# A graph network's edge sort: twelve of 28 blocks scattered by POOL's transfers, the layers' small additions apart, eight row buffers

## The chip, the cores and the metric

The kernel runs on one core of one Trainium2 chip. The metric is the time of one execution on the device, in microseconds.

## The reference

```python
# x: 12500 x 64, edges: 400000 with src, dst (sorted by dst), edge_weight
# attention layer
a = einsum('nd,hde->nhe', h, Wh)
attn = softmax(sum(a * h[:, None, :], -1) / sqrt(d), axis=0)
neigh = segment_sum(h[src][:, None, :] * attn[src][:, :, None], dst, n)
x = layernorm(x + elu(neigh.reshape(n, -1) @ weight))
# three message layers, then x = layernorm(x + h)
ef = concatenate([nf[src], nf[dst], traj[:, None]], -1)
msg = leaky_relu(ef @ We.T + be)
red = segment_sum(msg, dst, n)
h = leaky_relu(concatenate([nf, red], -1) @ Wn.T + bn)
```

## The kernel before

All gathers by node are made with one-hot matmuls on windows of 128 nodes (98 windows, `NW`). For that the edges are first put in the order of the source's window, and later, in quads of four slots, in the order of the target's window. The program runs through these stages one after the other.

**Sort** (the block at L482 to L757). The 3125 tiles of 128 edges are cut into 28 blocks of 115 tiles (the last has 20), and these into lots of five tiles, 23 lots a block, 625 in all. In a block every edge gets a rank, its place among 16384 slots of the block when it is ordered by window, with each window's part rounded up to runs of 16. SP loads a block's rows; PE turns them, ACT casts them (L513); DVE makes the fields (`fields_of`, L627). Then, by lots, DVE writes the one-hots of windows and segments (L667, L669), PE counts them (L554, L556) and, 29 lots later, adds up the ranks (L581 to L588), which DVE reads with a maximum (L701, 30 lots behind the one-hots) and, at the end of each group of eight lots, splits into column and row (`places`, L705). Ten lots later still (`LAG_GRID` 40) comes the grid: DVE writes one-hots of column and row (L721, L722) and four products of the column one-hot with fields (L725), ACT two more products for every tile (L521, `weigh`), and PE multiplies row one-hots with these (L602), so that a 128x128 grid of three fields fills in two banks. DVE reads it (L733, `read_grid`) and SP stores it in `runs` (L502). POOL does nothing in this stage. The order on each engine is that of the loops `for lot in steps_of`; semaphores count lots.

**Preparation** (L758 to L1217): where each run goes, gathers of runs by POOL (L1034), the fields of the slots (`make_meta`, L1037), the attention's scores.

**Source phase** (`source_phase`, L1257), once for the attention and once for each layer: 960 groups of 512 slots, two groups a transfer. SP loads the one-hots (`hits_s`, L1293) and POOL the side rows (L1331) three transfers ahead, ACT copies the group's window of the table (L1347), PE makes the products (L1368, L1373), DVE copies a bank into one of four row buffers `made` (L1396), and SP stores a buffer of two groups in `rows` (L1301). DVE may write into a buffer when its last store has landed. Each engine's loop has eight groups a turn (`laps`, L1224).

**Target phase** (`first_target_phase`, L1430, and `target_phase`, L1553, for the layers): 976 groups of 128 quads. POOL gathers the quads' rows (L1457, L1581). In a layer SP loads one-hots of two groups (L1591), PE makes the target's part (L1622), DVE adds it to the quads (`add`, L1654), applies the leaky rectifier (`leaky`, L1658), splits the message into three bfloat16 pieces (`less`, L1662, `split`, L1666), PE sums by node (L1426), and DVE adds the sums into `hr` (`keep`, L1673), one small addition a group, whose window comes from a register that is loaded at L1245. Each `keep` waits until the one before it has been written. Between layers stands `between`, L1755.

```python
            for p in range(pairs + 3):
                if p < pairs:
                    add(p)
                if 1 <= p <= pairs:
                    less(p - 1)
                if p < pairs:
                    leaky(p)
                if 1 <= p <= pairs:
                    split(p - 1)
                if p >= 3:
                    keep(2 * p - 6)
                    keep(2 * p - 5)
```

## Time and profile before

| | |
|---|---|
| median of 3 runs | 13272.0 us (13263.73 to 13275.16) |
| the profiled execution | 13268.24 us, its span 13266.9 us |
| busy: PE, DVE | 8804.1 us, 10738.3 us |
| busy: ACT, POOL | 5614.5 us, 5614.8 us |
| mean granted TensorE clock | 0.885 |
| DMA | 1931.77 MB in 1720140 packets, mean 146 GB/s |

Engines: PE is TensorE (PEld its weight loads), DVE VectorE, ACT ScalarE, POOL GpSimd, SP SyncE. A row of a group of instructions gives line, engine, operation, output and inputs, their number, then busy time and mean time of one, then the idle time of the engine before them and what ended it. A row of the timeline gives start, duration, engine, line, operation and, in brackets, the idle time before it.

### The profile page before, as it was taken

The numbers are of one execution on the slowest core, as the hardware profiler recorded it, in microseconds if no ns is written. First come the engines' busy times: TensorE is split into PE (matmuls) and PEld (weight loads), VectorE is DVE, ScalarE is ACT, GpSimd is POOL, SyncE is SP. The second block draws the span as 40 slices with busy tenths as digits, with TensorE's granted clock in tenths as the row PEclk, the third lists the DMA queues.
The fourth block names the chain that finished last, engine by engine and source line by source line (L and its number), as shares of the span: only waits on it lengthen the run. The fifth ranks groups of instructions, "written<-read, shape, count | busy, mean of one in ns | idle before, by whom it ended". The sixth has DMA issues, their size and how long they took to land. (4 is left out here: it accounts for less than half of the span.)

```text
span 13266.9 us, 519123 instructions
## 1 busy us (share of the span) xinstructions
PE 8804.1 (66%) x172644; PEld 7365.0 (56%) x172644; DVE 10738.3 (81%) x26542; ACT 5614.5 (42%) x15578; POOL 5614.8 (42%) x6333
## 2 busy tenths in 40 slices
PE   6777777766377666656765555777555567756556
PEld 4555555543366655556665555566555556655554
DVE  8999999986377799985569998555999965589997
ACT  4666666661133388764432222344222234422222
POOL 0000000017522377752346666234666633366663
PEclk9999999985555588868999999899999989999998
DMA  1000000002488767776875556587555558855555
GB/s 36 5 5 5 5 5 5 4 7 48 122 246 245 211 195 195 195 152 184 269 227 171 172 172 162 142 261 246 171 171 171 170 112 265 269 182 172 171 172 108
DMA packets 1720140, 1931.77 MB, mean 146 GB/s; under 512 B 256050, under 2 KB 1577028, under 8 KB 1719140
## 3 DMA queue, kind: packets, MB, share of 16 engines
q1 hardware_dynamic: 1458065, 1370.73, 34.0%
q0 software_dynamic: 261120, 548.82, 17.1%
q8 instruction: 238, 3.90, 0.1%
q10 hardware_dynamic: 304, 4.93, 0.1%
q14 instruction: 413, 3.38, 0.1%
HBM read 1202.74 MB, written 725.45 MB: 145 GB/s over the span
## 5 line engine op out<-in xcount | busy, mean ns | idle before, releaser
L1581 POOL DMA_INDIRECT work<-rows,quad_at x2928 | 3091.6, 1056 | 1490.4 <-DVE work L1654 1000.2
L1426 PE MATMUL bank<-work 128*128 128x64 bf16 x46848 | 2073.8, 199 | 1358.8 <-DVE hr L1673 1349.1
L1426 PEld LDWEIGHTS bank<-work 128*128 128x128 fp8e4 (+1 forms) x46848 | 1846.7, 102 | 1515.1 <-issue 1462.5
L1606 ACT COPY work<-tabs 128x192 bf16 x2928 | 1028.8, 351 | 3556.3 <-PE bank L1622 3231.4
L1396 DVE COPY work<-bank 128x256 f32<-128x256 f32 (+1 forms) x3840 | 1551.8, 422 | 1107.5 <-DMA rows<-work 625.1
L1373 PE MATMUL bank<-work 128*128 128x64 bf16 x46080 | 2412.7, 203 | 0.5 <-issue 0.5
L521 ACT ACTIVATE work<-work,tabs 128x128 bf16<-128x128 bf16 x6250 | 1919.2, 427 | 932.7 <-DVE work L721 932.7
L1347 ACT COPY work<-tabs 128x192 bf16 x3840 | 1349.0, 351 | 2108.0 <-PE bank L1373 1605.3
L1373 PEld LDWEIGHTS bank<-work 128*128 128x128 fp8e4 x46080 | 2167.6, 104 | 0.6 <-issue 0.6
L1331 POOL DMA_DIRECT2D side<-meta x1920 | 1071.5, 558 | 2301.9 <-PE bank L1373 2083.9
L1368 PE MATMUL bank<-wtraj,side 128*128 128x64 bf16 x11520 | 1558.1, 195 | 555.7 <-ACT work L1347 252.1
L1622 PE MATMUL bank<-work 128*128 128x64 bf16 x35136 | 1304.2, 195 | 541.8 <-DMA work<-hits_g 305.4
L1368 PEld LDWEIGHTS bank<-wtraj,side 128*128 128x128 bf16 x11520 | 1130.1, 98 | 764.3 <-DVE work L1396 519.6
L1622 PEld LDWEIGHTS bank<-work 128*128 128x128 fp8e4 x35136 | 1167.0, 99 | 673.2 <-issue 613.0
L602 PE MATMUL bank<-work 128*128 128x384 bf16 x9375 | 1290.6, 291 | 38.6 <-ACT work L521 38.6
L725 DVE TENSOR_TENSOR work<-work,tabs 128x768 bf16<-128x768 bf16 x2500 | 1222.0, 549 | 0.0
L778 POOL MEMSET tabs<- 128x976 f32 x1 | 0.9, 916 | 2871.5 <-DMA runs<-work 2871.5
L1457 POOL DMA_INDIRECT work<-rows,quad_at x976 | 984.6, 1009 | 416.4 <-PE bank L1426 228.5
L1654 DVE TENSOR_TENSOR work<-bank,work 128x512 f32<-128x512 f32 x1464 | 1012.8, 692 | 137.3 <-PE bank L1622 102.2
L602 PEld LDWEIGHTS bank<-work 128*128 128x128 bf16 x9375 | 825.1, 102 | 384.9 <-issue 56.9
L1658 DVE SCALAR_TENSOR_TENSOR work<-work 128x512 f32<-128x512 f32 x1464 | 1001.4, 684 | 0.1
L1666 DVE TENSOR_TENSOR work<-work 128x512 bf16<-128x512 f32 x1464 | 1000.9, 684 | 0.1
(324 smaller groups left out, 13996.5 us busy)
## 6 DMA issues: line engine op xcount, KB each, us to landing
work<-hits_g SPq DMA_DIRECT2D x1464, 256.0 KB
rows<-work SPq DMA_DIRECT2D x1440, 256.0 KB, 3.4
work<-hits_s SPq DMA_DIRECT2D x1440, 128.0 KB, 3.2
hits_g<-work SPq DMA_DIRECT2D x976, 128.0 KB
rows<-work SPq DMA_DIRECT2D x480, 260.0 KB, 4.9
work<-rows,quad_at POOLq DMA_INDIRECT x3904
work<-meta_src SPq DMA_DIRECT2D x480, 128.0 KB, 4.2
hits_s<-work SPq DMA_DIRECT2D x480, 128.0 KB, 4.6
```

The costliest lines, as they stand in the source:

```text
L521: last = sca.activation(values[lot % 3][:, f, j // 2, :, j % 2], of_tile(hit_col[lot % 3], j), ACT.Copy, scale=of[name][:, t:t + 1])
L602: last = ten.matmul(to[:, f * P:3 * P].rearrange("p (f c) -> p f c", c=P), of_tile(hit_row[lot % 3], j), v[:, fields[0]:fields[1], j // 2, ...
L725: last = vec.tensor_tensor(values[at][:, f, :, :, :], hit_col[at], twos(lot, name, P), ALU.mult)
L1331: pool.dma_start(side[0:high - low, n % 4, :, :], meta[bass.ds(l * GROUP_LOT, GROUP_LOT), low:high, :].rearrange("g r s -> r g s")).then_i ...
L1347: sca.copy(window[q % 8].unsqueeze(1), tabs[:, 0, bass.ds(w, 1), :]).then_inc(s_window, 1)
L1368: ten.matmul(home, beside, wtraj[:, :], start=True, stop=False, skip_group_check=True)
L1373: last = ten.matmul(home, hits[n][:, q % GROUP_LOT, slots], window[q % 8][:, k * D:(k + 1) * D], start=False, stop=k == 2, skip_group_chec ...
L1396: vec.tensor_copy(made[n][:, q % GROUP_LOT, :], bank[q % 8][:, 0:QUAD * width]).then_inc(s_read, 1)
L1426: last = ten.matmul(to[:, 0:D], hits_of(j), piece_of(j), start=j == 0 and k == 0, stop=j == QUAD - 1 and k == 2, skip_group_check=True)
L1581: pool.indirect_dma_start(quads[g // 2 % (GATHERED // 2)][:, half(g)], None, table, bass.IndirectOffsetOnAxis(ap=quad_at[:, g:g + 1], axis ...
L1606: sca.copy(window[q % 4].unsqueeze(1), tabs[:, 1, bass.ds(w, 1), :]).then_inc(s_window, 1)
L1622: last = ten.matmul(to[:, j * D:(j + 1) * D], hits_t[:, j * P:(j + 1) * P], window[q % 4][:, k * D:(k + 1) * D], start=k == 0, stop=k == 2 ...
```

## The change

1. Blocks 0, 2, ... 22 (`by_pool`) do not go through the grid. DVE writes their fields as records (source low part + 1, target, weight) in one of four record buffers and turns the ranks into slot numbers with one instruction per group of places. POOL then issues one indirect transfer of 128 records of 12 bytes per tile into a table of that block in DRAM, `runs_of`, and, when the next such block is through, one transfer that copies the table into `runs`. SP fills these twelve tables with blanks first. The other sixteen blocks use the grid as before, counted among themselves (`grid_no`). All engines wait at the end for the grid's stores and for `s_moved`.
2. A run's layout is now slot by slot (`e f`) instead of field by field (`f e`), in the grid read, the blanks and `make_meta`.
3. In the source phases there are eight row buffers (`MADE`) and sixteen groups a turn.
4. In the target phases of the layers the two small additions stand apart.

```diff
+    by_pool = lambda b: b % 2 == 0 and b < 24
+    RECORDS = 4
+    record = [room.cut(3 * BT).rearrange("p (t f) -> p t f", f=3) for _ in range(RECORDS)]
+    slot = [room.cut(BT).bitcast(I32) for _ in range(RECORDS)]
+    runs_of = {b: dram(f"runs_of_{b}", [BLOCK_RUNS, 3 * RUN], F32) for b in pool_blocks}
+    @block.gpsimd
+    def _(pool):
+        pool.wait_ge(*edges_here)
+        pool.wait_ge(s_blanked, 16 * len(pool_blocks))
+        def move(k):
+            b = pool_blocks[k]
+            pool.wait_ge(s_scattered[k % RECORDS], 16 * BT * (k // RECORDS + 1))
+            pool.dma_start(in_rows(runs[b * BLOCK_RUNS:(b + 1) * BLOCK_RUNS, :]), in_rows(runs_of[b])).then_inc(s_moved, 16)
+        for n, (first, end) in enumerate(place_groups):
+            b = group_block[n]
+            if by_pool(b):
+                k = pool_blocks.index(b)
+                way = k % RECORDS
+                to = runs_of[b].rearrange("r (e f) -> (r e) f", f=3)
+                pool.wait_ge(s_slots, kind_no(n) + 1)
+                for t in range(tile(first, 0), tile(end - 1, LOT - 1) + 1):
+                    pool.indirect_dma_start(to, bass.IndirectOffsetOnAxis(ap=slot[way][:, t:t + 1], axis=0),
+                                            record[way][:, t, :], None).then_inc(s_scattered[way], 16)
+                if end == blocks[b][1] and k >= 1:
+                    move(k - 1)
+        move(len(pool_blocks) - 1)
...
     def _(syn):
         syn.wait_ge(*edges_here)
+        syn.wait_ge(*blanks_ok)
+        for b in pool_blocks:
+            syn.dma_start(in_rows(runs_of[b]), blanks.rearrange("p s f -> p (s f)")).then_inc(s_blanked, 16)
...
         def fields_of(b):
+            if by_pool(b):
...
+                at_least(vec, s_scattered[k % RECORDS], 16 * BT * (k // RECORDS))
+                vec.tensor_copy(record[k % RECORDS][:, :, 1], turn_bank[:, BT:2 * BT])
+                vec.tensor_copy(record[k % RECORDS][:, :, 2], weight)
+                vec.tensor_scalar(record[k % RECORDS][:, :, 0], low_i[:, 0:BT], 1.0, None, ALU.add)
...
         def places(n):
             vec.wait_ge(s_rank, end)
+            if by_pool(b):
+                vec.tensor_scalar(slot[pool_blocks.index(b) % RECORDS][:, a:z], rank_f[b % 2][:, a:z], -float(BIG), None,
+                                  ALU.add).then_inc(s_slots, 1)
+                return
...
-            if here(lot - LAG_GRID):
+            if in_grid(lot - LAG_GRID):
                 spread(lot - LAG_GRID)
...
     for e in (nc.vector, nc.scalar, nc.tensor, nc.sync, nc.gpsimd):
         for n in range(2):
-            e.wait_ge(s_stored[n], 16 * NB // 2)
+            e.wait_ge(s_stored[n], 16 * len(grid_blocks) // 2)
+        e.wait_ge(s_moved, 16 * len(pool_blocks))
...
+        MADE = 8
+        around = MADE * GROUP_LOT
-        made = [room.cut(GROUP_LOT * QUAD * width).rearrange("p (g c) -> p g c", g=GROUP_LOT) for _ in range(4)]
+        made = [room.cut(GROUP_LOT * QUAD * width).rearrange("p (g c) -> p g c", g=GROUP_LOT) for _ in range(MADE)]
-            laps(vec, NS, step)
+            laps(vec, NS, step, around)
...
                     add(p)
+                if p >= 3:
+                    keep(2 * p - 6)
                 if 1 <= p <= pairs:
                     less(p - 1)
+                if p >= 3:
+                    keep(2 * p - 5)
                 if p < pairs:
                     leaky(p)
                 if 1 <= p <= pairs:
                     split(p - 1)
-                if p >= 3:
-                    keep(2 * p - 6)
-                    keep(2 * p - 5)
```

The order on DVE in the target phase of a layer, before the change; `TENSOR_LOAD win_g` is the register load of a small addition, `ISA` belongs to its address:

```order
 L1673 TENSOR_TENSOR hr<-hr,bank 128x64
 L1245 TENSOR_LOAD win_g
 L1673 ISA
 L1673 TENSOR_TENSOR hr<-hr,bank 128x64
 L1654 TENSOR_TENSOR work<-bank,work 128x512
 L1662 TENSOR_TENSOR work<-work 128x512
 L1658 SCALAR_TENSOR_TENSOR work<-work 128x512
 L1666 TENSOR_TENSOR work<-work 128x512
```

The same place after the change (L1736 is the addition of the quads, L1744, L1740 and L1748 are the old L1662, L1658 and L1666, L1755 is the small addition):

```order
 L1736 TENSOR_TENSOR work<-bank,work 128x512
 L1322 TENSOR_LOAD win_g
 L1755 ISA
 L1755 TENSOR_TENSOR hr<-hr,bank 128x64
 L1744 TENSOR_TENSOR work<-work 128x512
 L1322 TENSOR_LOAD win_g
 L1755 ISA
 L1755 TENSOR_TENSOR hr<-hr,bank 128x64
 L1740 SCALAR_TENSOR_TENSOR work<-work 128x512
 L1748 TENSOR_TENSOR work<-work 128x512
```

One of the two additions and its load moved ahead of the subtraction, the other behind it.

The order on POOL in the sort after the change, where before it had no instruction between L369 and L778; L530 is the scatter of one tile's records (230 for blocks 0 and 2 together), L520 the move of a finished block:

```order
 L369 MEMSET marker 1x1
 L416 MEMSET tabs 128x128x2
 L417 MEMSET tabs 128x128
 L511 UNCONDITIONAL_BRANCH
 L530 DMA runs_of<-tabs 16384x3 x230
 L520 DMA runs<-runs_of 16x3072
 L530 DMA runs_of<-tabs 16384x3 x115
 L520 DMA runs<-runs_of 16x3072
```

A block's 115 scatters stand between two moves, and the move of a block stands behind the scatters of the next one.

## Rows read from the trace of the kernel before

**Rows 1.** The page: busy time of engines, and DVE's busy tenths in 40 slices

```profile
PE 8804.1 (66%) x172644; PEld 7365.0 (56%) x172644; DVE 10738.3 (81%) x26542; ACT 5614.5 (42%) x15578; POOL 5614.8 (42%) x6333
...
DVE  8999999986377799985569998555999965589997
```

**Rows 2.** Busy time by stage; last columns granted clock, DMA share, GB/s

```profile
54.00:2919.00 2865.00, 2117.62 (x23346) 1592.93 (x23346) 2840.62 (x6737) 1925.91 (x6276) 0.52 (x1) 0.95 0.02 5
3491.00:4531.00 1040.00, 782.51 (x15331) 715.27 (x15328) 739.57 (x1916) 333.94 (x951) 279.40 (x476) 0.55 0.85 245
...
6087.00:6820.00 733.00, 560.84 (x15343) 493.26 (x15340) 379.42 (x960) 334.50 (x952) 260.87 (x476) 0.99 0.87 268
6832.00:8323.00 1491.00, 878.56 (x22937) 784.90 (x22937) 1355.45 (x2872) 335.52 (x955) 1016.05 (x963) 0.98 0.61 169
8474.00:9227.00 753.00, 569.22 (x15341) 497.38 (x15338) 386.04 (x960) 334.43 (x952) 260.96 (x476) 0.99 0.85 261
...
10882.00:11622.00 740.00, 569.41 (x15337) 500.48 (x15334) 381.39 (x960) 334.23 (x952) 260.89 (x476) 0.99 0.86 266
```

**Rows 3.** Timeline of DVE in the sort, before the grid's first lot

```profile
90.72 0.67 DVE L701 TENSOR_REDUCE work<-bank 128x5 f32<-128x490 f32 x1 [1.13 <-PE bank L588]
...
93.76 0.67 DVE L701 TENSOR_REDUCE work<-bank 128x5 f32<-128x490 f32 x1
```

**Rows 4.** Timeline of DVE in the sort, a lot with grid work

```profile
155.50 0.66 DVE L701 TENSOR_REDUCE work<-bank 128x5 f32<-128x490 f32 x1
...
157.01 1.96 DVE L725 TENSOR_TENSOR work<-work,tabs 128x768 bf16<-128x768 bf16 x4
...
159.72 0.66 DVE L701 TENSOR_REDUCE work<-bank 128x5 f32<-128x490 f32 x1
```

**Rows 5.** Grouped instructions: POOL's indirect transfers

```profile
L1581 POOL DMA_INDIRECT work<-rows,quad_at x2928 | 3091.6, 1056 | 1490.4 <-DVE work L1654 1000.2 <-issue 490.2
...
L1191 POOL DMA_INDIRECT marks_g<-later_home x98 | 116.4, 1188 | 33.9 <-issue 33.9
L898 POOL DMA_INDIRECT marks_s<-tabs x28 | 27.1, 966 | 19.0 <-DVE tabs L906 10.7 <-issue 8.2
```

**Rows 6.** Timeline of DVE in a layer's target phase, one iteration

```profile
7500.80 0.68 DVE L1662 TENSOR_TENSOR work<-work 128x512 f32<-128x512 f32 x1
7501.40 0.69 DVE L1658 SCALAR_TENSOR_TENSOR work<-work 128x512 f32<-128x512 f32 x1
7502.00 0.69 DVE L1666 TENSOR_TENSOR work<-work 128x512 bf16<-128x512 f32 x1
7502.60 0.21 DVE L1673 TENSOR_TENSOR hr<-hr,bank 128x64 f32 x1
7503.04 0.22 DVE L1673 TENSOR_TENSOR hr<-hr,bank 128x64 f32 x1 [0.22 <-DVE hr L1673]
...
7503.85 0.68 DVE L1662 TENSOR_TENSOR work<-work 128x512 f32<-128x512 f32 x1
```

**Rows 7.** Timeline of POOL in the same iteration

```profile
7501.15 1.16 POOL L1581 DMA_INDIRECT work<-rows,quad_at  x1 [0.63 <-DVE work L1654]
7502.62 0.96 POOL L1581 DMA_INDIRECT work<-rows,quad_at  x1 [0.30 <-issue]
```

**Rows 8.** Grouped instructions: small additions, and PE's target part in the layers

```profile
L1622 PE MATMUL bank<-work 128*128 128x64 bf16 x35136 | 1304.2, 195 | 541.8 <-DMA work<-hits_g 305.4 <-DVE work L1654 198.2 <-issue 3.9
...
L1673 DVE TENSOR_TENSOR hr<-hr,bank 128x64 f32 x2928 | 634.4, 217 | 337.1 <-DVE hr L1673 337.1
```

**Rows 9.** The layers' source phases: grouped instructions, and a window as in rows 2

```profile
L1396 DVE COPY work<-bank 128x256 f32<-128x256 f32 x2880 | 1147.4, 422 | 1104.7 <-DMA rows<-work 625.1 <-PE bank L1373 444.0
L1368 PEld LDWEIGHTS bank<-wtraj,side 128*128 128x128 bf16 x11520 | 1130.1, 98 | 764.3 <-DVE work L1396 519.6 <-issue 155.2 <-ACT work L1347 42.4
...
6294.00:6306.00 12.00, 9.27 (x290) 8.61 (x286) 6.80 (x18) 5.62 (x16) 4.91 (x9) 1.00 0.95 300
```

**Rows 10.** Grouped instructions: the grid read

```profile
L733 DVE TENSOR_SCALAR work<-bank 128x128 f32<-128x128 f32 x84 | 19.0, 279 | 3.4 <-PE bank L602 3.4
```

More of the change, by code:

```diff
@@ L450, in build @@
     s_stored = [sort(f"grid_stored{n}") for n in range(2)]
+    s_blanked, s_slots, s_moved = sort("blanked"), sort("slots"), sort("moved")
+    s_scattered = [sort(f"scattered{n}") for n in range(RECORDS)]
     place_groups = []
@@ L480, in ends_block, with in_grid, grid_no, kind_no @@
         return block_of(lot) if here(lot) and lot + 1 == blocks[block_of(lot)][1] else None
+    def in_grid(lot):
+        return here(lot) and not by_pool(block_of(lot))
+    def grid_no(lot):
+        return sum(1 for k in range(lot) if in_grid(k))
+    def kind_no(n):
+        return sum(1 for k in range(n) if by_pool(group_block[k]) == by_pool(group_block[n]))
     block = nc.Block()
     block.__enter__()
+    @block.gpsimd
[19 more added lines that the diff above has]
+        move(len(pool_blocks) - 1)
     @block.sync
@@ L617, in _ @@
                 rank(lot - LAG_RANK + 1)
-            if here(lot - LAG_GRID - 1):
+            if in_grid(lot - LAG_GRID - 1):
                 grid(lot - LAG_GRID - 1)
@@ L629, in fields_of @@
             vec.wait_ge(s_turned, b + 1)
-            if b >= 4:
-                vec.wait_ge(s_grid, blocks[b - 4][1])
+            if b >= 4 and not by_pool(b - 4):
+                vec.wait_ge(s_grid, grid_no(blocks[b - 4][1]))
             wide = lambda ap: ap[:, 0:2 * BT].rearrange("p (f t) -> p f t", f=2)[:, :, 0:n]
@@ L751, in _ @@
                     places(group_ends[lot - LAG_RANK])
-            if here(lot - LAG_GRID):
+            if in_grid(lot - LAG_GRID):
                 spread(lot - LAG_GRID)
-            if (b := ends_block(lot, LAG_GRID + 2)) is not None:
+            if (b := ends_block(lot, LAG_GRID + 2)) is not None and not by_pool(b):
                 read_grid(b)
@@ L1222, in build, with laps @@
     LAP = 8
-    def laps(engine, count, step):
-        for q in range(LAP):
+    def laps(engine, count, step, size=LAP):
+        for q in range(size):
             step(q, q, 0)
-        with engine.Fori(1, count // LAP - 1) as i:
-            for q in range(LAP):
-                step(i * LAP + q, q, i)
-        for g in range(count - LAP, count):
-            step(g, g % LAP, g // LAP)
+        with engine.Fori(1, count // size - 1) as i:
+            for q in range(size):
+                step(i * size + q, q, i)
+        for g in range(count - size, count):
+            step(g, g % size, g // size)
     serial = itertools.count()
@@ L1318, in _ @@
                 load(l, l)
[L1319 removed]
+            laps(syn, NS, step, around)
             for l in range(lots - 2, lots):
@@ L1375, in step @@
                 last.then_inc(s_rows, 1)
-            laps(ten, NS, step)
+            laps(ten, NS, step, around)
         @block.vector
```

110 lines of the change are left out of this document (66 added, 44 removed).

## The prediction, made before the changed kernel was run

> **What bounds the kernel now.** I read the engines' shares first, then busy time by stage, then the grouped instructions of the stages that the change touches, then single iterations in the timeline. Over the whole span DVE is busiest, 81%, but its share by slice runs from 9 down to 3 [rows 1], so no engine bounds everything. The stages differ [rows 2]:
>
> - The sort, from 54 to 2919 us, has DVE busy 2840.6 of 2865.0 us, POOL with one instruction and DMA at a share of 0.02. It is DVE's alone.
> - Each of the three layers' source phases takes 733 to 753 us. DVE is busy only about half of it and PE three quarters, and DMA has a share of 0.85 to 0.87 at 261 to 268 GB/s: transfers and waits for them.
> - Each target phase takes about 1490 us, with DVE busy 1355.45 of 1491. It is DVE's again, with gaps.
>
> **The sort on DVE.** Before the grid starts, a lot costs DVE two one-hots and one rank read: the rank reads at 90.72 and 93.76 stand two lots apart, so 1.52 us a lot [rows 3]. With the grid's two one-hots and four products the next rank read comes 4.22 us later (155.50 to 159.72), and the four products alone fill 1.96 us [rows 4]. A block scattered by POOL drops these six, so a lot saves 4.22 - 1.52 = 2.70 us. Twelve blocks of 23 lots are 276 lots: 745 us. Each such block also drops the three instructions of its grid read, nine of twelve on places (three in each of three groups) and five of thirteen on fields. At the grid read's 0.279 us [rows 10] these 17 are at most 4.7 us a block, at least 0; they overlap in part and I take 2.5, in all 30 us. Against it stand twelve blank fills that are queued on SP ahead of the first block's loads; 12 x 196 KB at the 245 GB/s that DMA moved in the first source phase [rows 2] are 10 us. So DVE would end the sort 745 + 30 - 10 = 765 us earlier, at 2919 - 765 = 2154 us. ACT (ten weighings a lot) and PE (the grid's matmuls) only lose work there; DVE, busy 2840.6 of 2865.0 us, hardly waits for them, so that is worth nothing.
>
> **The sort on POOL.** POOL gets 12 x 115 = 1380 scatters of 128 records of 12 bytes. The trace has no such scatter. Nearest are the marks: 98 records take 0.966 us and about 0.30 us until the next, 125 records take 1.188 us and 33.9/98 = 0.35 us; the gathers of 128 rows take 1.056 us in the mean [rows 5]. That brackets one scatter between 0.95 + 0.30 = 1.25 us and 1.19 + 0.35 = 1.54 us when nothing disturbs it. Something does: in the target phase the gather that starts while DVE runs L1662 takes 1.16 us, the one that starts beside L1666's end and L1673 takes 0.96 us [rows 6, 7]. The first gets going when L1662 ends, although L1658 has already started, so it waits for one DVE instruction with two SBUF inputs, 0.2 us here. In the sort DVE runs such instructions nearly without a break, each 0.55 us long and begun every 0.47 us, so a scatter waits 0 to 0.43 us, some 0.2 us in the middle. I take 0.96 + 0.20 + 0.30 = 1.46 us less a little for the rank reads, which read PSUM, so 1.44 us; ends 1.25 and 1.54 + 0.2 = 1.74 us. POOL's first slots are ready when eight lots are ranked, near 105 to 110 us. Then it ends at 110 + 1380 x 1.44 + 12 us for the twelve moves of finished blocks = 2109 us. DVE's 2154 is later, so **DVE still bounds the sort**, by only 45 us. At 1.25 us POOL ends at 1847 and nothing changes; at 1.74 us it ends at 2523, and the sort saves 396 instead of 765 us. POOL becomes the bound from (2154 - 122) / 1380 = 1.47 us on. Four record buffers let POOL lag three of its blocks before DVE's field step waits, so DVE need not stop. The new waits on POOL have nothing else queued behind them, and the moves wait for scatters of the block before, long landed. DMA had a share of 0.02, so the records' traffic is hidden.
>
> The new layout of runs makes the later DVE reads step 12 bytes; they stepped before too. Priced at 0, bounds -5 to +20 us for some 100 instructions of the preparation stage.
>
> **The layers' small additions.** In a target iteration the first addition into hr starts at 7502.60 and lasts 0.21, the second starts at 7503.04: 0.22 us are idle, released by the first one [rows 6]. Over 2928 additions that idle time is 337.1 us [rows 8]. After the change a subtraction of 0.6 us lies between them, as the order of the instructions shows, and the window's register load still has an instruction to run under. The iteration goes from 3.05 (7500.80 to 7503.85) to 2.82 us; 1464 x 0.23 = 337 us. What may be late next: a pair's two gathers now need 1.16 + 0.30 + 0.96 + 0.30 = 2.72 us [rows 7], and if both meet a blocking instruction 2.92; and the loads of hits_g, for which PE waits 305.4 us already [rows 8], are issued after a scatter that is now released by the last split of an iteration instead of the first addition. I give back 37 us: **300 us**, ends 0 and 337.
>
> **Eight row buffers.** In the source phases DVE waits 625.1 us for stores of rows to land [rows 9], 208 us of about 740 a phase. That is not the gain, because DMA is at 0.87. After a stall, 12 us ran at a share of 0.95 and 300 GB/s [rows 9], against 268 in the mean. So at most 733 x (1 - 268/300) = 78 us a phase, 235 in all, at least 0. I take halfway to 300, 284 GB/s: 733 x (1 - 268/284) = 41 us a phase, 124 in all. The loops' bodies double too, which halves the turns. PE's weight loads of the three phases wait 155.2 us for nothing that the profile shows [rows 9]; half of it, 78, is the most that fewer turns can give, 0 the least, and I take 26. Together **150 us**. The first source phase waits little for stores of rows; 0.
>
> **Sum.** 765 + 300 + 150 = 1215 us off the profiled execution's own 13268.2 us (span 13266.9): 12053, say **12050 us**. The median of the runs shown, 13272.0, lies 4 us above that execution, which changes nothing.
>
> **The rivals.**
> *POOL bounds the sort.* For it: my 1.44 and the crossing at 1.47 us nearly touch, and a scatter of 125 records took 1.54. Against: 98 records and gathers of 128 rows run at 1.26. At 1.60 us POOL ends at 122 + 2208 = 2330, 176 us after DVE: 12050 + 176 = 12226, about 12230 us.
> *Layers give little.* DMA at 0.87 is already the ceiling, and in the target phase half of the 300 us comes back as waits for hits_g or for gathers. For it: PE's 305.4 us and the thin POOL margin. Against: the 300 GB/s stretch. Then 12050 + 150 + 150 = 12350 us.
> *Slower.* A scatter waits not for one DVE instruction but for the whole unbroken run, so that one gets through per rank read. A lot with grid work is 4.22 us, one without 1.52; at 3.0 us a scatter POOL ends the sort at 122 + 4140 = 4262, 1343 later than now, and the total is 13268 + 1343 - 450 = 14160 us. It turns the sign from (2919 + 450 - 122) / 1380 = 2.35 us a scatter on. Against it is the gather that got in between L1662 and L1658 [rows 6, 7]. The Trainium skill's page "SBUF — State Buffer", section "Who interferes with whom", says that a VectorE instruction with two SBUF inputs and a GpSimd instruction that reads SBUF exclude each other, and that the loser is fully blocked. The trace agrees on the blocking, and shows it ending with the one instruction.
> *It doesn't do what it says.* The scatter's slots would come so late that grid and scatter run one after the other, or the gap between additions is the register load's: no gain over 0.2%.
>
> **How the numbers follow.** Forecast 50%, POOL-bound 20%, layers give little 24%, slower 4%, nothing 2%. A measurement of this kernel can tell about 0.2%, 27 us. Faster 0.94, same 0.02, slower 0.04. The range: down by 85 us for the source phases' end, 37 for the target phases', and some 60 for the small terms, 11870; up it takes in POOL at 1.60 us and the poor layers (12350) with 100 us of POOL's lag on top, 12450.
>
> **What would show it.** Right: the sort ends near 2150 us with DVE at 9 throughout, POOL's scatters 1.15 us each, 1.44 us apart, done some tens of us before DVE; in the target phase no idle time released by the other addition and 2.82 us between two additions from the bank; in the source phases the wait of DVE for rows gone, DMA over 0.9, some 690 us each. Wrong: a last wait of the sort for POOL's moves with DVE idle; DVE in the target phase waiting for PE behind hits_g; source phases still 733 us with PE waiting for its loads.

## The result, and the profile after

The changed kernel takes 12440.2 us (median of 4 runs, 12430.95 to 12460.75) against 13271.2 us (4 runs, 13263.73 to 13275.16) of the kernel before: a ratio of 0.9377, 95% interval 0.936 to 0.9393. The profiled execution took 12460.75 us, its span is 12459.6 us. That is 807 us less than the profiled execution before. I had forecast 1215 us less. The median lies in my range, 10 us below its upper end of 12450; the profiled execution lies 11 us above it.

The page, engines' busy time and the slices, answers to [rows 1]:

```profile
PE 8132.3 (65%) x168504; PEld 6910.0 (55%) x168504; DVE 9842.5 (79%) x24682; ACT 4777.9 (38%) x12818; POOL 7654.0 (61%) x7727
...
DVE  8997779634677799986569999555999965589997
POOL 5888888877322477762347777233777733367774
```

DVE's row begins with 8997779 where it stood at 9 before, and POOL is at 8 over the same slices: the sort is no longer DVE's alone. Busy time by stage (sort, first source phase, a source and a target phase of the first layer, the two other source phases), as in [rows 2]:

```profile
54.00:2574.00 2520.00, 1592.80 (x19209) 1244.60 (x19209) 2049.08 (x4877) 1080.03 (x3519) 2007.66 (x1393) 0.87 0.04 6
...
3149.00:4195.00 1046.00, 775.32 (x15344) 710.46 (x15342) 739.61 (x1916) 334.31 (x952) 280.13 (x476) 0.57 0.85 243
5751.00:6469.00 718.00, 556.16 (x15347) 494.06 (x15344) 405.95 (x959) 334.51 (x952) 262.06 (x476) 0.99 0.88 274
6480.00:7858.00 1378.00, 854.65 (x23291) 770.15 (x23288) 1313.94 (x2914) 340.29 (x968) 1029.71 (x972) 0.97 0.66 185
7984.00:8715.00 731.00, 570.28 (x15336) 500.99 (x15334) 406.25 (x959) 334.35 (x952) 262.04 (x476) 0.98 0.87 269
10231.00:10958.00 727.00, 569.31 (x15347) 500.23 (x15344) 407.33 (x960) 334.50 (x952) 262.05 (x476) 0.99 0.87 271
```

From the first and last instructions of each stage in the two traces:

| stage | before, us | after, us | difference | forecast |
|---|---|---|---|---|
| end of the sort | 2918.5 | 2573.7 | -344.8 | -765 |
| three source phases of the layers | 2224.3 | 2175.9 | -48.4 | -150 |
| three target phases of the layers (first to last large addition) | 4554.0 | 4134.2 | -419.8 | -300 |
| all the rest | | | +5.5 | 0 |

So three terms of the sum were off, and they partly cancel: 420 us too much in the sort, 102 too much in the source phases, 120 too little in the target phases.

**The sort after.** The scatters as one line's instructions (smallest, median and largest duration in ns, first and last start):

```profile
L530 POOL DMA_INDIRECT runs_of<-tabs x1380: 956/1007/5911, 108.5 to 2568.0; - x198
its engine sat idle before it (us, times) until:
  issue: 454.2, 1379
  DVE tabs L781: 61.4, 1
who waited for it (us, times):
  DVE tabs L699: 204.7, 5
```

POOL scatters from 108.5 us up to the end of the sort. It waited for DVE once, 61.4 us before the first scatter, and then only its own 0.3 us between two (3 us where a move stands between them): it is the bound. The median, 1.007 us, is below the 1.16 I had forecast; the mean is 2000.5 / 1380 = 1.450 us, because there is a second kind. DVE waits too, 204.7 us in five places, for a record buffer that POOL has not emptied. At the end of the sort it stands idle for 200.75 us:

```profile
2575.98 0.07 DVE L866 MEMSET tabs<- 1x16 f32 x1 [200.75 <-POOL tabs L859]
```

So DVE was through at 2375.2 us, and without the 204.7 us of waiting it would have been at 2170.5. Here is the second kind, in the timeline of POOL and, for the same time, of DVE (start, duration, engine, line):

```profile
2098.91 3.92 POOL L530 DMA_INDIRECT runs_of<-tabs  x1 [0.30 <-issue]
2103.13 3.92 POOL L530 DMA_INDIRECT runs_of<-tabs  x1 [0.30 <-issue]
```

```profile
2098.26 0.55 DVE L796 TENSOR_TENSOR work<-lane_pairs,tabs 128x768 bf16<-128x768 bf16 x1
2098.73 0.55 DVE L797 TENSOR_TENSOR work<-lane_pairs,tabs 128x768 bf16<-128x768 bf16 x1
2099.20 1.96 DVE L800 TENSOR_TENSOR work<-work,tabs 128x768 bf16<-128x768 bf16 x4
2101.07 0.46 DVE L737 TENSOR_TENSOR tabs<-lane_pairs,tabs 128x588 bf16<-128x588 bf16 x1
2101.45 0.55 DVE L739 TENSOR_TENSOR work<-lane_pairs,tabs 128x750 bf16<-128x750 bf16 x1
2101.91 0.67 DVE L771 TENSOR_REDUCE work<-bank 128x5 f32<-128x490 f32 x1
```

The scatter that starts at 2098.91, 0.18 us into the second one-hot (L797), is done at 2102.83. That is 0.83 us after the last instruction with two SBUF inputs, L739, has ended (2101.45 + 0.55 = 2102.00). One gets through per lot of 4.22 us. Other scatters end 0.83 us after the one DVE instruction that they met: 1.10 us is the usual length of one that starts in a later L800. Counted over the records of L530, 206 of 1380 took more than 2 us, 3.765 us in the mean, and 1174 took 1.043 us in the mean. Each of the 206 ends 0.83 to 0.88 us after the last instruction with two SBUF inputs of an unbroken run (L739, or the last L800 in lots without one-hots), none after one in the middle of a run. The longest, 5.91 us, met a run of twelve, two lots' grid work with no reduction between. The 206 cost 206 x (3.765 - 1.043) = 561 us of POOL's time. Without them POOL would have been done near 2007 us, ahead of DVE.

**The target phases after**, the timeline of DVE over one iteration, answers to [rows 6]:

```profile
7001.78 0.68 DVE L1736 TENSOR_TENSOR work<-bank,work 128x512 f32<-128x512 f32 x1
7002.38 0.21 DVE L1755 TENSOR_TENSOR hr<-hr,bank 128x64 f32 x1
7002.51 0.68 DVE L1744 TENSOR_TENSOR work<-work 128x512 f32<-128x512 f32 x1
7003.11 0.21 DVE L1755 TENSOR_TENSOR hr<-hr,bank 128x64 f32 x1
7003.24 0.68 DVE L1740 SCALAR_TENSOR_TENSOR work<-work 128x512 f32<-128x512 f32 x1
```

and the grouped instructions, to [rows 8]:

```profile
L1704 PE MATMUL bank<-work 128*128 128x64 bf16 x35136 | 1300.6, 195 | 1033.9 <-DMA work<-hits_g 1017.9 <-issue 11.0 <-DVE work L1736 3.4
...
L1736 DVE TENSOR_TENSOR work<-bank,work 128x512 f32<-128x512 f32 x1464 | 1005.0, 686 | 219.8 <-PE bank L1704 194.5 <-DMA work<-rows,quad_at 13.2 <-PE bank L1508 0.9
...
L1755 DVE TENSOR_TENSOR hr<-hr,bank 128x64 f32 x2928 | 617.9, 211 | 11.1 <-PE bank L1508 6.4 <-DVE hr L1755 0.9
```

The wait of 337.1 us is gone. The next instruction also starts 0.13 us after a small addition, not 0.21: its last 0.08 us now lie under the next one. PE's wait for hits_g has grown from 305.4 to 1017.9 us, and 194.5 us of it reach DVE.

**The source phases after**, answers to [rows 9]:

```profile
L1449 PE MATMUL bank<-wtraj,side 128*128 128x64 bf16 x11520 | 1555.3, 196 | 514.6 <-ACT work L1427 264.8 <-DVE work L1478 113.2 <-DMA side<-meta 79.6
L1449 PEld LDWEIGHTS bank<-wtraj,side 128*128 128x128 bf16 x11520 | 1132.4, 98 | 715.7 <-DVE work L1478 270.3 <-ACT work L1427 264.2 <-issue 115.2
```

DVE's wait for rows to land (625.1 us) is gone, but PE's weight loads sit idle nearly as long as before (715.7 against 764.3 us), now partly for ACT's window copies.

### The profile page after: what moved, and what is told of

It is laid out like the page before. It is cut to its first block and busy times, and to the rows that moved or that the text cites. A ratio compares the mean times of both kernels' runs of the same rounds, so it can differ in the third digit from the quotient of the medians.

```text
span 12459.6 us, 502768 instructions
## 1 busy us (share of the span) xinstructions
PE 8132.3 (65%) x168504; PEld 6910.0 (55%) x168504; DVE 9842.5 (79%) x24682; ACT 4777.9 (38%) x12818; POOL 7654.0 (61%) x7727
## 5 line engine op out<-in xcount | busy, mean ns | idle before, releaser
L1454 PE MATMUL bank<-work 128*128 128x64 bf16 x46080 | 2405.8, 203 | 0.2 <-issue 0.2
L1478 DVE COPY work<-bank 128x256 f32<-128x256 f32 (+1 forms) x3840 | 1625.9, 424 | 986.8 <-PE bank L1454 895.2
L1508 PE MATMUL bank<-work 128*128 128x64 bf16 x46848 | 1943.9, 199 | 574.4 <-DVE work L1748 568.6
L530 POOL DMA_INDIRECT runs_of<-tabs x1380 | 2000.5, 1450 | 515.6 <-issue 454.2
L1508 PEld LDWEIGHTS bank<-work 128*128 128x128 fp8e4 (+1 forms) x46848 | 1747.0, 102 | 696.0 <-issue 673.9
L1704 PE MATMUL bank<-work 128*128 128x64 bf16 x35136 | 1300.6, 195 | 1033.9 <-DMA work<-hits_g 1017.9
L577 ACT ACTIVATE work<-work,tabs 128x128 bf16<-128x128 bf16 x3490 | 1071.1, 427 | 1219.9 <-DVE work L796 1219.9
L1449 PEld LDWEIGHTS bank<-wtraj,side 128*128 128x128 bf16 x11520 | 1132.4, 98 | 715.7 <-DVE work L1478 270.3
L1736 DVE TENSOR_TENSOR work<-bank,work 128x512 f32<-128x512 f32 x1464 | 1005.0, 686 | 219.8 <-PE bank L1704 194.5
L1744 DVE TENSOR_TENSOR work<-work 128x512 f32<-128x512 f32 x1464 | 1000.7, 684 | 1.3
L1740 DVE SCALAR_TENSOR_TENSOR work<-work 128x512 f32<-128x512 f32 x1464 | 1000.1, 683 | 0.1
L1748 DVE TENSOR_TENSOR work<-work 128x512 bf16<-128x512 f32 x1464 | 999.3, 683 | 0.0
L1451 PE MATMUL bank<-ones_b,side 128*128 128x1 bf16 x3840 | 692.6, 187 | 452.2 <-DVE work L1470 201.3
L610 PE MATMUL bank<-work,tabs 128*98 128x125 bf16 x3125 | 431.9, 231 | 683.6 <-DVE work L739 676.2
```

The source lines that it names most:

```text
L530: pool.indirect_dma_start(to, bass.IndirectOffsetOnAxis(ap=slot[way][:, t:t + 1], axis=0), record[way][:, t, :], None).then_inc(s_scattere ...
L577: last = sca.activation(values[n % 3][:, f, j // 2, :, j % 2], of_tile(hit_col[n % 3], j), ACT.Copy, scale=of[name][:, t:t + 1])
L1449: ten.matmul(home, beside, wtraj[:, :], start=True, stop=False, skip_group_check=True)
L1454: last = ten.matmul(home, hits[n][:, q % GROUP_LOT, slots], window[q % 8][:, k * D:(k + 1) * D], start=False, stop=k == 2, skip_group_chec ...
L1478: vec.tensor_copy(made[n][:, q % GROUP_LOT, :], bank[q % 8][:, 0:QUAD * width]).then_inc(s_read, 1)
L1508: last = ten.matmul(to[:, 0:D], hits_of(j), piece_of(j), start=j == 0 and k == 0, stop=j == QUAD - 1 and k == 2, skip_group_check=True)
```

## The experiments

My theory after the result: POOL bounds the sort, through scatters that are held by a whole run of DVE instructions with two SBUF inputs; the target phases' gain belongs to the small additions alone; the source phases are close to what the transfers allow. Each step is tried by itself. Numbers are from one profiled execution each where no interval is given. Beside the first three kernels below the kernel before took 13255.5 us; beside the three cuts, the ten blocks and the two deeper loads 13262.7; beside the single cut, the control, the halved stores and the first combination 13319.2, 0.4% more on the chip of the same number as 13262.7, for which I have no reason; beside the last 13250.1.

**The small additions alone**, in the kernel before:

```diff
                     add(p)
+                if p >= 3:
+                    keep(2 * p - 6)
                 if 1 <= p <= pairs:
                     less(p - 1)
+                if p >= 3:
+                    keep(2 * p - 5)
...
-                if p >= 3:
-                    keep(2 * p - 6)
-                    keep(2 * p - 5)
```

> The kernel before with one part of the change alone: in the target phases of the layers the two small additions of a pair stand apart (the first behind the pair's addition, the second behind the first subtraction). If this part alone carries the gain of the target phases, each of the three falls from about 1518 to about 1378 us, as in the changed kernel, the wait of the small addition falls from 337 us to under 30 us, the sort (end at 2918), the first source phase (1040) and the layers' source phases (732 to 752) stay, and the whole is near 12,850 us. Rival: part of the 420 us comes from the rest of the change (other row buffers, other places in SBUF, rows already written when the phase begins); then the phases stay above 1420 us and the whole above 12,970 us.

Measured: 12822.0 us, 433.5 less than before. The target phases took 1375.8, 1371.3 and 1372.2 us, the small addition's wait fell to 9.5 us, the sort stayed, and the layers' source phases took 9 us less together though nothing was changed in them. Its grouped instructions show the same new wait of PE as the changed kernel:

```profile
L1622 PE MATMUL bank<-work 128*128 128x64 bf16 x35136 | 1300.6, 195 | 1018.5 <-DMA work<-hits_g 1002.9 <-issue 12.8 <-DVE work L1654 0.5
...
L1673 DVE TENSOR_TENSOR hr<-hr,bank 128x64 f32 x2928 | 613.7, 210 | 9.5 <-PE bank L1426 4.7 <-DVE hr L1673 1.2
```

So the whole gain of the target phases is this part's, and it is more than half of what the change gives.

**The eight row buffers alone**, in the kernel before:

```diff
+        MADE = 8
+        around = MADE * GROUP_LOT
-        made = [... for _ in range(4)]
+        made = [... for _ in range(MADE)]
-            laps(vec, NS, step)
+            laps(vec, NS, step, around)
```

> The kernel before with eight row buffers (and sixteen groups a turn) in the source phases, nothing else changed. If the 48 us that the layers' source phases lost belong to this part, they become 718 to 732 us each, VectorE's wait for a row buffer disappears (625 us over the program in the kernel before), the target phases stay at 1516 to 1520 us, and the whole is near 13,220 us. Rival one: VectorE's wait was on the path as I forecast, and something else in the changed kernel ate the gain; then the phases come near 690 us each and the whole near 13,120 us. Rival two: the eight buffers give nothing and the 48 us come from elsewhere; then the whole stays within 15 us of the kernel before.

Measured: 13232.6 us, 22.9 less. The layers' source phases took 711.8, 734.3 and 733.1 us, 45 us less together; the first source phase took 9 us more and the target phases 6 us more. The DMA share stands where it stood in the changed kernel, 0.86 to 0.88. The first expectation holds within some 3 us a phase: the 45 to 48 us are this part's but for the 9 us that these phases moved by themselves in the kernel above, and nothing else in the changed kernel ate a larger gain.

**A fifth of the scatters**, in the changed kernel (the counts that two waits expect fall with them):

```diff
-                for t in range(tile(first, 0), tile(end - 1, LOT - 1) + 1):
+                for t in range(tile(first, 0), tile(end - 1, LOT - 1) + 1, 5):
```

> The changed kernel, with POOL scattering only every fifth tile of each of its twelve blocks: 276 scatters instead of 1380. It leaves out four fifths of the records of these blocks. VectorE's work is the same. If POOL bounds the sort of the changed kernel, and VectorE would be done at my 2154 us, the sort ends between 2130 and 2230 us instead of at 2574, and the whole falls by the same 340 to 440 us to 12,020 to 12,110 us. Rival: it is VectorE's own term that was wrong (its instructions take longer beside the scatters, or it waits for PE or for loads), and POOL only follows; then the sort still ends after 2400 us.

Measured: 12043.2 us, sort end 2171.8 us, POOL's last scatter at 1762 us (20 of its 276 are held as well). DVE's work in the sort is that of the changed kernel (x4877 in both windows), in 402 us less:

```profile
54.00:2172.00 2118.00, 1598.93 (x19209) 1248.28 (x19209) 2045.02 (x4877) 1080.03 (x3519) 336.94 (x289) 0.94 0.03 7
```

So POOL's scatters are the whole difference, and my 2154 us for DVE was right to 18 us.

**Cuts in DVE's run.** Three memsets of two columns per grid lot, in the changed kernel:

```diff
+    gap, turns = room.cut(128), itertools.count()
+    def cut_run(vec):
+        vec.memset(gap[:, 2 * (next(turns) % 64):][:, 0:2], 0.0)
...
             vec.tensor_tensor(hit_row[at], columns(P), twos(lot, "row", P), ALU.is_equal)
+            cut_run(vec)
...
                 last = vec.tensor_tensor(values[at][:, f, :, :, :], hit_col[at], twos(lot, name, P), ALU.mult)
+                if f == 1:
+                    cut_run(vec)
             last.then_inc(s_vector_values, 1)
+            cut_run(vec)
```

> The changed kernel with three VectorE memsets of two columns in each grid lot, which stand between its instructions that read two operands from SBUF: so the unbroken run of these, some 4 us, is cut into four pieces of 0.7 to 1.5 us. Added for VectorE: 276 x 3 x about 0.06 us, some 50 us, which alone would put its own end at about 2220 us (2172 in the kernel with a fifth of the scatters). If a scatter that begins beside this run is held until the run ends (206 of 1380 take over 2 us, mostly 3.92 us), the cuts let it through earlier: few or none above 2.3 us, the mean falls from 1.45 us to 1.1 to 1.25 us, and the sort ends between 2250 and 2400 us, by 170 to 320 us earlier. Rival one: a cut by a memset frees nothing (a scatter gets through only where VectorE reads PSUM, or waits); then the long ones stay at about 200 of 3.9 to 4.1 us, and the sort ends at 2574 to 2640 us. Rival two: the long ones are a matter of POOL's own queue (a full ring, a late transfer) and have nothing to do with VectorE; then their number and length stay too, and they no longer end with VectorE's last subtraction of a lot.

Measured: 12074.5 us, sort end 2188.6 us, the last scatter issued at 2169.4; 37 scatters above 2 us. The scatters of this kernel, grouped:

```profile
L534 POOL DMA_INDIRECT runs_of<-tabs x1380 | 1597.1, 1157 | 520.6 <-issue 458.3 <-DVE tabs L785 62.3
```

The gain is larger than expected, since DVE ends the sort only 17 us after the end it had with a fifth of the scatters. The memsets are 62.8 us busy but lie partly beside their neighbours. The 37 show that such a memset does not always let a scatter through: 27 of them were held across all three, 9 across two, and all 37 end where the run ends. Is it the place of the cuts, or their number? Two more kernels ask that.

**One cut in place of three**, the middle one (behind `f == 1`):

> The changed kernel with one of the three memsets in each grid lot, the middle one, between the second and third product: the unbroken run of eight instructions becomes one of four (2.2 us) and one of four (2.1 us). If a scatter is let through at the cut, and one that begins in the first part waits at most some 2.3 us, no scatter is near 3.9 us any more except where the run is longer than a lot's, and the sort ends between 2170 and 2300 us. Rival: what frees a scatter is a short piece (a single instruction or two), and one cut leaves most of the held ones held, now for 2 to 2.5 us; then over 200 of them are above 1.6 us and the sort ends between 2300 and 2450 us.

Measured: sort end 2211.5 us, 12168.8 us in all (beside 13319.2), 65 scatters above 2 us, 34 of them above 3 us where I had expected hardly any; the end of the sort is as expected. This kernel shows a release at the cut. Timeline of POOL, and of DVE from the same lot:

```profile
252.89 2.15 POOL L534 DMA_INDIRECT runs_of<-tabs  x1 [0.30 <-issue]
```

```profile
253.19 1.49 DVE L804 TENSOR_TENSOR work<-work,tabs 128x768 bf16<-128x768 bf16 x3
254.15 0.06 DVE L453 MEMSET work<- 128x2 f32 x1
```

The second product starts 0.47 us after the first and lasts 0.55, so it ends near 254.21, where the cut is; the scatter ends at 255.04, 0.83 us later. 29 of the 65 end so, at the cut; the other 36 were held across it and end with the run. Of the 88 scatters that start 150 to 190 ns into the second one-hot, 28 end like this one, 40 end after one instruction (1.2 us), and 20 are held for 3 us or longer in spite of the cut. In the changed kernel 148 of 149 that start there are held.

**The same three memsets where the run ends anyway**, just ahead of `read_rank` (the control):

```diff
             if here(lot - LAG_RANK):
+                if in_grid(lot - LAG_GRID):
+                    for _ in range(3):
+                        cut_run(vec)
                 read_rank(lot - LAG_RANK)
```

> The changed kernel with the same three memsets of two columns in each grid lot as in the kernel with the cuts (x1047, 63 us of VectorE), but all three together just ahead of the reduction of the ranks, where the unbroken run ends anyway. If it is the place of the memsets that freed the scatters, nothing is freed here: about 200 or more of the scatters stay at 3.9 us, and the sort ends at 2560 to 2660 us. Rival: the memsets help by their mere number (they slow VectorE and shift its turns against POOL's); then the number above 2 us falls to under 100 here too, and the sort ends below 2400 us.

Measured: 12144.5 us (beside 13319.2), sort end 2188.7 us. My expectation failed and the rival held. The scatters:

```profile
L534 POOL DMA_INDIRECT runs_of<-tabs x1380: 954/1097/2476, 110.7 to 2071.8; - x198
```

Not one is held for a whole run, although the run has no cut. Timelines of POOL and of DVE for one lot:

```profile
1505.17 1.23 POOL L534 DMA_INDIRECT runs_of<-tabs  x1 [0.30 <-issue]
1506.71 1.10 POOL L534 DMA_INDIRECT runs_of<-tabs  x1 [0.31 <-issue]
1508.12 1.00 POOL L534 DMA_INDIRECT runs_of<-tabs  x1 [0.30 <-issue]
```

```profile
1503.49 0.54 DVE L743 TENSOR_TENSOR work<-lane_pairs,tabs 128x750 bf16<-128x750 bf16 x1
1503.98 0.06 DVE L453 MEMSET work<- 128x2 f32 x1
1503.98 0.66 DVE L775 TENSOR_REDUCE work<-bank 128x5 f32<-128x490 f32 x1
...
1505.02 0.55 DVE L801 TENSOR_TENSOR work<-lane_pairs,tabs 128x768 bf16<-128x768 bf16 x1
```

The scatter at 1505.17 starts 0.15 us into the second one-hot and is through after 1.23 us. POOL's pattern now repeats with the lot, three scatters each, and falls a few tens of ns earlier against DVE: of those that start in the second one-hot, 85 lie 100 to 149 ns into it, 0 held. In the changed kernel 149 lie 150 to 199 ns into it, and 148 of them are held. So a run of DVE holds a scatter only in some alignments of the two engines, and memsets get rid of the held ones in two ways: by a release at the cut, which the kernel with one cut shows, and by something that works from outside the run as well, a shift of the pattern or a change of how DVE takes up its next instruction. How much of the gain of the three cuts is the one and how much the other I can't say, and why so small a shift should decide stays open.

**Ten blocks instead of twelve** on POOL (`b < 20`), in the changed kernel:

> The changed kernel with ten of the 28 blocks on POOL instead of twelve; the two others go back to the grid. POOL: (2568 - 108) / 12 = 205 us a block, so ten end near 2160 us by themselves. VectorE: 2172 us where POOL held nothing up (a fifth of the scatters), and 69 us for each of two more grid blocks, so 2310 us. Each engine's work then fits below the other's, and VectorE is the bound: the sort ends between 2290 and 2350 us, the whole falls by 225 to 285 us to 12,155 to 12,235 us. Rival: POOL's time is no sum of its own scatters but is made by the grid lots beside it (a held scatter for each run of VectorE), and VectorE waits for record buffers in turn, so that fewer blocks on POOL help less; then the sort ends above 2400 us.

Measured: 12300.7 us, sort end 2414.2 us. Fewer scatters, and yet more of them held: 258 of 1150 above 2 us, and a higher mean:

```profile
L530 POOL DMA_INDIRECT runs_of<-tabs x1150 | 1917.8, 1668 | 439.8 <-issue 378.4
```

The 258 take 976 us, 703 us more than they would at the 1.056 us of the others; without that POOL would have been done near 1706 us, ahead of the 2310 that I had drawn up for DVE. DVE, too, waited 108.6 us for record buffers and was through at 2405; less that wait it is at 2297, as drawn up. The rival stands: POOL's price per block isn't its own, it is made by the grid lots beside it.

**Eight buffers of hits in the layers' target phases**, in the changed kernel, sixteen groups a turn:

```diff
-        hits_home = [... for _ in range(4)]
+        hits_home = [... for _ in range(DEEP)]
...
-                at_least(syn, s_sum, 2 * (p - 3), since)
+                at_least(syn, s_sum, 2 * (p - DEEP + 1), since)
...
-            for p in range(3):
+            for p in range(DEEP - 1):
```

> The changed kernel with eight instead of four buffers for the hits of a pair in the layers' target phases, loaded seven pairs ahead instead of three. If PE's 1018 us of waiting at the first product is the short lead of these loads (a load is issued when the pair three ahead of it has been summed, and lands 3 us later), most of this wait goes, and the excess at the end of each phase (45 us above the steady 2.67 us a pair) with it: each target phase falls from 1378 to 1310 to 1345 us, the whole by 100 to 200 us. Rival: the pace of 2.67 us is POOL's (two gathers of 1.33 us from start to start, no idle time), and the excess at the end is the transfers' own time, whatever their lead; then PE's wait turns into another one, the median stays at 2.67 us, and the phases stay within 15 us of 1378.

Measured: the target phases took 1342.1, 1340.9 and 1340.9 us, 110 us less together; the total, 12378.7, falls by 61.5 us and not by the 100 to 200 expected, because its sort ended at 2598.7 us (218 scatters held). PE's wait is gone, and no other took its place on PE:

```profile
L1705 PE MATMUL bank<-work 128*128 128x64 bf16 x35136 | 1307.6, 195 | 67.1 <-DMA work<-hits_g 33.6 <-issue 23.6 <-DVE work L1737 0.5
```

So the short lead of the loads was the cause. (The loop's turns were doubled in the same edit; no run has that alone. It is the wait for hits_g that went, from 1017.9 to 33.6 us.) What is left over DVE's own 1301 us a phase is 40 us.

**Eight buffers of hits and side values in the layers' source phases** (loads seven lots ahead instead of three, `hits_home` and `side` eight deep), in the changed kernel:

> The changed kernel with eight instead of four buffers for the hits and for the side values in the layers' source phases, loaded seven lots ahead instead of three. If PE waits there for loads that were issued too late, the phases fall by 20 us or more each (718 to 732 us now). Rival, which I hold likelier: PE's waits for the loads are small (some 80 us over three phases for the side values), and the pace is set by the chain of ACT's windows, PE's products and VectorE's copy, or by what the 16 DMA engines can move at a share of 0.88; then the phases stay within 10 us.

Measured: 713.0, 731.7 and 723.2 us, 8 us less together, where the small additions alone, which change nothing in them, had moved them by 9; the whole took 12455.2 us. The rival holds: the lead of these loads isn't what bounds there.

**Half of the row stores** in the second and third layer's source phases, in the changed kernel:

```diff
-                syn.dma_start(to_rows[:, bass.ds(l * GROUP_LOT, GROUP_LOT), :], made[n % MADE])
+                syn.dma_start(to_rows[:, bass.ds(l * GROUP_LOT, 1 if number > 1 else GROUP_LOT), :], made[n % MADE][...])
```

> The changed kernel, storing in the source phases of the second and third layer only one of each two groups' rows. It leaves out half of the rows that the second and third layer's target phases gather (they read older ones). If the pace of the source phases is what the 16 DMA engines can move (share 0.88, 271 to 275 GB/s now, of which the stores are the larger part), these two phases fall from 731 and 726 us to 550 to 650 us. Rival: the pace is the chain of ACT's window copy, PE's products and VectorE's copy of the sums, and the DMA engines merely keep up; then the two phases stay within 15 us of 731 and 726 while the DMA share falls.

Measured, first the layer that stores all, then the two that store half:

```profile
5808.00:6527.00 719.00, 556.23 (x15337) 496.00 (x15335) 404.96 (x959) 334.49 (x952) 260.93 (x476) 0.98 0.88 273
8050.00:8689.00 639.00, 520.27 (x15353) 480.70 (x15350) 403.37 (x960) 334.57 (x952) 260.88 (x476) 0.98 0.72 210
10215.00:10848.00 633.00, 517.73 (x15351) 476.86 (x15348) 402.98 (x960) 334.69 (x953) 260.93 (x476) 0.99 0.73 212
```

The first expectation holds (550 to 650 us). The two phases fall by about 93 us against the 731 and 726 of the changed kernel, and the share from 0.87 to 0.72: the transfers are on the path. They aren't all of it, for at a share of 0.72 the phase still takes 633 us.

**Combinations.** The first has the three cuts, the deep hits, and the moves of finished blocks on SP:

> The changed kernel with the three cuts, with the eight buffers of hits in the layers' target phases, and with the moves of POOL's finished blocks issued by SP, eight blocks later, instead of by POOL (each cost POOL a gap of 3 us). From the two kernels measured apart: 12,075 us with the cuts less 3 x 36 us of the target phases is 11,965 us. The moves: POOL ends its last scatter at 2169 us in the kernel with the cuts and VectorE is as late, so taking 36 us from POOL gives 0 to 15 us. I expect 11,950 to 11,970 us, a ratio of 0.901 to 0.903 to the kernel before. Rival: the moves on SP's queue hold back its loads of coming blocks (a move waits for the last scatter), and the sort ends later than 2188 us.

Measured: 12021.9 us (4 runs) beside 13319.2 (7 runs), ratio 0.9022 [0.9007, 0.9037]; as expected in the ratio, while the time itself is 52 us above what I had expected. The sort ends at 2188.4 us: the moves on SP gave nothing, as DVE is the bound. The second has the three memsets ahead of `read_rank`, the deep hits and the deep source loads:

> The changed kernel with the three memsets just ahead of the reduction of the ranks (the place where they were meant to free nothing, and where one scatter of 1380 took over 2 us), with the eight buffers of hits in the layers' target phases, and with the eight buffers of hits and side values in the layers' source phases; POOL keeps its moves. If the effects add up: sort end 2189 us as before with either set of memsets (VectorE is its bound, POOL's last scatter at 2072 us), target phases near 1342 us, source phases 713 to 735 us, so a ratio of 0.901 to 0.903 to the kernel before, the same as the kernel with the cuts and the deep hits within 0.1%. If the freedom from held scatters was luck of where POOL's scatters happened to start, a new layout may bring them back: then over 100 of them take more than 2 us again, and the sort ends after 2300 us.

Measured: 11932.2 us (4 runs) beside 13250.1 (7 runs), ratio 0.9009 [0.8994, 0.9024]. No scatter is above 2 us, the sort ends at 2186.6 us, the target phases take 1340.2, 1339.0 and 1339.2 us:

```profile
L534 POOL DMA_INDIRECT runs_of<-tabs x1380: 957/1099/1952, 110.1 to 2080.4; - x198
```

This kernel also narrows the open question of the control. 25 of its scatters start 150 to 159 ns into the second one-hot, and none is held; of those that start in these 10 ns, both are held in the changed kernel and 5 of 7 in the first combination. So to within 10 ns the place of the start alone does not decide.

Both beat the changed kernel (0.9377) by nearly 4%. The intervals of the two overlap.

## Why the prediction was right or wrong

The total is inside the range partly by luck: the sort lost 420 us of its forecast gain, more than the 176 + 100 us that the upper end allowed for it, and the layers, for which it took off 300 us, together gave 18 us more than forecast. Two of the signs of being wrong that I had named are in the trace: DVE idle at the end of the sort (200.75 us), and DVE waiting for PE behind hits_g (194.5 us).

- **"DVE would end the sort at 2154 us"**: right. 2171.8 us with a fifth of the scatters.
- **"A scatter waits for one DVE instruction; I take 1.44 us"**: this is the step that failed. It measured (2568.0 - 108.5) / 1379 = 1.78 us from start to start, above even my upper end of 1.74. For 1174 scatters the step was right and even too dear (1.04 + 0.30 = 1.34 us). For 206 it was wrong: they wait for several DVE instructions in a row, up to the end of the run. I had this mechanism among the rivals, as "slower", and ruled it out with one gather that got in between two instructions of the target phase. One row can show that something happens, not that it always does. The outcome lies between two of my cases: POOL-bound by its time, and held by the run for one scatter in seven. The sum behind my crossing of 1.47 us held: 122 + 1380 x 1.78 = 2578 us, measured 2574.
- **"So DVE need not stop", with four record buffers**: wrong once POOL lags: DVE waited 204.7 us at the field step. It cost nothing by itself: POOL waited for DVE only before its first scatter, and DVE was through 200 us before the sort ended.
- **The small additions, 300 us**: right mechanism, undersized: 420 us. I counted the idle 0.22 us, and not that the addition's own tail then lies under the next instruction (0.13 instead of 0.21 us, twice an iteration; 2928 x 0.08 = 234 us at most). The iteration measured 2.67 us in the median, not 2.82 (2.83 in the mean, with its waits; before, 3.05 and 3.12). Of the 337 + 234 = 571 us, some 150 came back: 110 of them as waits for hits_g, which I had named as next late and priced within 37.
- **Gathers, "2.72 us a pair"**: they need 2.67 us, as much as the iteration. With the two additions apart they take 1.03 us in the iteration shown and 1.06 in the mean; with the deep hits DVE waits 88.7 us for them over the three phases, more than for PE.
- **Eight row buffers, 150 us**: 48 us. The working was sound and the size a choice: "halfway to 300 GB/s" became 269 to 274 GB/s. With the measured 274 my own formula gives 733 x (1 - 268/274) = 16 us a phase, and the phases lost 14, 21 and 13. The doubled bodies took the 155.2 us that the weight loads waited for nothing visible to 115.2; the phases' time, as the formula gives it without them, shows none of these 40 us.
- **Preparation and first source phase at 0**: 4 and 6 us more, within my bounds for the first.
- **The skill's rule.** The Trainium skill, page "SBUF — State Buffer", section "Who interferes with whom", says that a `tensor_tensor` with both inputs in SBUF contends with GpSimd's reads. Its section "SBUF: two separate sides" says of such an instruction that whoever starts first has the shared pair "for the whole instruction" and that the other fully blocks. The trace agrees on the blocking (3.92 us against 1.04). On its end it shows both: releases at the end of the one instruction, and 206 scatters held beyond it, all of them to the end of the run.

## What to carry to other kernels

Where DVE runs instructions with two SBUF inputs back to back, price an indirect transfer of POOL at both ends: to the end of one instruction and to the end of the run. The difference here was 561 us of POOL's time. When work is moved to POOL, look at the distribution of its durations, not at the mean; a median of 1.0 and a mean of 1.45 us is a second kind of event, and a tiny instruction of another kind within or beside the run (here 60 ns, three a lot) can take most or all of it away, though why it does when it stands beside the run is open. When a stall in a loop goes, lengthen the lead of the loads in the same edit: the lead that covers 3.05 us an iteration did not cover 2.67.

## What the runs showed of the hardware that I had not expected

- A POOL transfer can be held by DVE for much longer than one instruction: 3.77 us in the mean for 206 of 1380 transfers, and every one of them ends 0.83 to 0.88 us after the last instruction of the run with two SBUF inputs. The same holds for the 258 with ten blocks and the 218 with the deep hits.
- Whether one is held turns on tens of nanoseconds of its start. Around 0.17 us into the second one-hot nearly all are held in the changed kernel; around 0.14 us into it none is, in the kernel with the memsets ahead of the rank read. Between 150 and 159 ns both of the changed kernel's are held and none of the 25 of the last combination, so the place alone doesn't decide. What does, I don't know.
- Three DVE memsets of 60 ns a lot, 62.8 us of busy time, moved the end of the sort by only 17 us where nothing else held it (2171.8 to 2188.6).
- Between the end of one scatter and the start of the next lie 0.30 us, whatever DVE does: 454.2 us over 1379 gaps in the changed kernel, the longer gaps at the moves included (0.33 in the mean with them), and 454.7 in the control.
